# Moving the stores of the whole rows from SyncE's queue to ScalarE's queue in the node stage of a graph kernel

## The chip, the cores and the metric

The kernel runs on one NeuronCore of one Trainium2 chip. The metric is the device time of one execution in microseconds (us). Engines are named as the profile names them: PE is TensorE (PEld its weight loads), DVE is VectorE, ACT is ScalarE, POOL is GpSimd, SP is SyncE. SPq and ACTq are the instruction streams of SP and ACT where they issue DMAs.

## The reference, cut to what matters

The layer is a gated graph convolution over 16 images (called b) of 1024 nodes with 256 features.

```python
pre_u = jnp.einsum('bud,dk->buk', h_t, W1[:d])
pre_v = jnp.einsum('bvd,dk->bvk', h_t, W1[d:])
hidden = jax.nn.relu(pre_u[:, :, None, :] + pre_v[:, None, :, :] + b1)
S = jax.nn.sigmoid(jnp.einsum('buvk,ko->buvo', hidden, W2)[..., 0] + b2[0])
a_t = jnp.einsum('buv,bud->bvd', S * A_a, h_t)
m_t = jnp.einsum('uv,bud->bvd', A_m, h_t) * h_t
z_t = beta1 * h_t + beta2 * (jnp.einsum('bvd,de->bve', a_t, Wa) + ba) + beta3 * (jnp.einsum('bvd,de->bve', m_t, Wm) + bm)
```

`h_t` is the input x, float32 (16, 1024, 256), and `A_a` and `A_m` are both the sparse input adj, (1024, 1024). The gate S is wanted only where adj is not zero, so the kernel computes it for the edges alone.

## The kernel before, in words

The kernel has a short setup, then the **node stage** (from about 52 us to about 1,410 us of the profiled execution), the edge stage (to about 3,600 us), which gathers rows of pre_u and pre_v by matrix products with selection matrices and reduces them to gates, and a last stage that applies the gates. Only the node stage is touched by the change. Stages are parted by a barrier of all engines.

The node stage loops over the 16 images b. In each image a **row phase** comes first: for the eight tiles t of 128 nodes (g = 8b + t numbers them over all images)

- PE multiplies the turned image by both halves of W1 (w = 0 and 1, two products of 128x274 each, four instructions of the trace per half), L561, into the two banks `ring0` and `ring1`. It waits until the bank's last contents were copied out (`ring_free`).
- ACT copies bank 0 to `whole[:, g % RW, 0, :]` (L640), DVE adds the bias to bank 1 and writes `whole[:, g % RW, 1, :]` (L723). RW is 3: `whole` and `split` have three slots, so tile g may not be written before the stores of tile g - 3 have landed. Both engines wait for that on `rows_stored`.
- `high` on ACT (L631, a CAST in the trace) rounds the whole values to the high part of a pair; `low` on DVE (L678) takes the rest. They lag by one tile: ACT does copy(t), then high(t - 1); DVE does copy(t), low(t - 1), take_own(t - 2) (L684).
- POOL adds the two halves for the gates of nodes with themselves (L813) and takes some columns.
- SP, in `store_rows`, waits for low of the tile (`low_ready`) and issues four stores: rows_dram from `split` (256 KB, then 288 KB, L461) and whole_dram from `whole` (128 KB, then 144 KB, L464). Each of the four adds 16 to `rows_stored` of the slot; the slot is free at 64 more.

After the row phase come the products with the adjacency (L577, `wide`), among which the sorting of edges is placed by a fixed schedule (PE: `rank_pair` L520 and `index_pair`; DVE: `start_pick`, `pick_u`, `pick_v`, and in some images a scan, L741), then hWa (L599, copied by ACT at L647), the turning of the next image (L510), and the product with Wm (L616, added to `base` by DVE at L794). Then the next image's row phase starts. In its own stream SP stores the pick matrices (L475), fills gate_dram with zeros (L478), stores hWa and base (L481, L484: 1 MB each) and loads the image after next (L455, 1 MB), all in program order; the last two stand directly ahead of the next row phase's stores.

The order of all this is the order of the code; there is no planner.

Of the kernel before, what the change touches and what calls it, by code (L numbers as in the profile page):

```python
# [5 lines left out]
def gnn_edges_kernel(nc, x, adj, W1, b1, W2, b2, Wa, ba, Wm, bm, beta1, beta2, beta3, out):  # L6
# [17 lines left out]
    P = 128  # L24
# [18 lines left out]
    LATE = D // 2  # L43
    EARLY = CG - LATE
    EG = EARLY // GW
    E0 = B * LATE
# [16 lines left out]
    whole_rows = whole_dram.rearrange("(n w) k -> n w k", w=2)  # L63

    ctx = ExitStack()
    with ctx:
        def sb(name, shape, dt=fp32, scope=ctx):
            return scope.enter_context(nc.sbuf_tensor(name, shape, dt))
# [4 lines left out]
        def sem(name):  # L73
            return ctx.enter_context(nc.semaphore(name))

        def waits(eng, sem_, value):
            if not isinstance(value, int) or value > 0:
                eng.wait_ge(sem_, value)
# [49 lines left out]
        with ExitStack() as phase:  # L128
# [216 lines left out]
            RW, RPK = 3, 4  # L345
# [5 lines left out]
            whole = sb("whole", [P, RW, 2, CW], scope=phase)  # L351
# [37 lines left out]
            rows_stored = [sem(f"rows_stored{i}") for i in range(RW)]  # L389
# [37 lines left out]
            def pairs_of(b):  # L427
                return range(min(max(PER * (b - 2), 0), PAIRS), min(max(PER * (b - 1), 0), PAIRS))

            def tile_at(b):  # L430
                return FIRST.index(b) if b in FIRST else None
# [19 lines left out]
            with nc.Block() as block:  # L451
                @block.sync
                def _(sp):
                    def load_h(b):
                        sp.dma_start(h[b % 2][:], x[b, :, :].rearrange("(t p) d -> p t d", p=P)).then_inc(h_loaded[b % 2], 16)  # L455

                    def store_rows(b, t):
                        g = b * NT + t
                        sp.wait_ge(low_ready, g + 1)
                        for at, wd, first in ((b * LATE, LATE, 0), (E0 + b * EARLY, EARLY, LATE)):  # L460
                            sp.dma_start(rows_dram[t * P:(t + 1) * P, :, :, at:at + wd].rearrange("p w q k -> p (w q) k"),  # L461
                                         split[:, g % RW, :, :, first:first + wd].rearrange("p w q k -> p (w q) k")
                                         .bitcast(fp32)).then_inc(rows_stored[g % RW], 16)
                            sp.dma_start(whole_rows[t * P:(t + 1) * P, :, at:at + wd],  # L464
                                         whole[:, g % RW, :, first:first + wd]).then_inc(rows_stored[g % RW], 16)

                    for b in range(2):
                        load_h(b)
                    sp.wait_ge(zero_set, 1)
                    for b in range(B):  # L470
                        for t in range(NT):
                            store_rows(b, t)
                        for p_ in pairs_of(b):
                            sp.wait_ge(v_picked, unit_of[p_] + 1)
                            sp.dma_start(pick_dram[2 * p_:2 * p_ + 2, :, :].rearrange("h v k -> (h v) k"),  # L475
                                         pick[p_ % RPK][:].bitcast(fp32)).then_inc(pick_stored[p_ % RPK], 16)
                        for z in range(ZPER):
                            sp.dma_start(gate_fill[b * ZPER + z, :, :], zero[:]).then_inc(zero_stored, 16)  # L478
                        for i in range(2):
                            sp.wait_ge(ring_free[i], USES * b + NT + 2)  # L480
                        sp.dma_start(hWa_dram[b, :, :].rearrange("(t p) d -> p t d", p=P), hWa[:]).then_inc(hWa_stored, 16)  # L481
                        for i in range(2):
                            sp.wait_ge(ring_free[i], USES * (b + 1))
                        sp.dma_start(base_dram[b, :, :].rearrange("(t p) d -> p t d", p=P), base[:]).then_inc(base_stored, 16)  # L484
                        if b + 2 < B:
                            load_h(b + 2)
                    sp.wait_ge(slot_free, B * NT)
                    for w in range(2):
                        for q in range(HALVES):
                            sp.dma_start(rows_dram[:, w, q, L0:ROW].rearrange("(t p) b -> p t b", p=P),  # L490
                                         linear[:, :, w, q, :].bitcast(fp32)).then_inc(linear_stored, 16)
                        sp.dma_start(whole_rows[:, w, L0:ROW].rearrange("(t p) b -> p t b", p=P),
                                     linear_whole[:, :, w, :]).then_inc(linear_stored, 16)
                    for i in range(RW):
                        sp.wait_ge(rows_stored[i], 64 * ((B * NT - i + RW - 1) // RW))
                    sp.wait_ge(linear_stored, 16 * 2 * (HALVES + 1))
                    sp.wait_ge(zero_stored, 16 * ZROWS)
                    sp.wait_ge(hWa_stored, 16 * B)
                    sp.wait_ge(base_stored, 16 * B)
                    for i in range(RPK):  # L500
                        sp.wait_ge(pick_stored[i], 16 * ((PAIRS - i + RPK - 1) // RPK))
# [119 lines left out]
                @block.scalar  # L621
                def _(act):
                    def take_turned(b):
                        act.wait_ge(hT_psum, b * DT + 1)
                        nc.scalar.copy(hT[:, 0, :], wide[:, 0:N]).then_inc(hT_ready, 1)

                    def high(b, t):
                        g = b * NT + t
                        for i in range(2):
                            act.wait_ge(ring_free[i], USES * b + t + 1)  # L630
                        nc.scalar.copy(split[:, g % RW, :, 0, :], whole[:, g % RW, :, :]).then_inc(high_ready, 1)  # L631

                    take_turned(0)
                    for b in range(B):
                        for t in range(NT):
                            g = b * NT + t
                            act.wait_ge(ring_full[0], USES * b + t + 1)
                            waits(act, rows_stored[g % RW], 64 * (g // RW))
                            waits(act, slot_free, g - RW + 1)
                            nc.scalar.copy(whole[:, g % RW, 0, :], ring[:, 0:CW]).then_inc(ring_free[0], 1)  # L640
                            if t >= 1:
                                high(b, t - 1)
                        high(b, NT - 1)
                        waits(act, hWa_stored, b * 16)
                        for i in range(HT):
                            act.wait_ge(ring_full[i % 2], USES * b + NT + i // 2 + 1)
                            nc.scalar.copy(hWa[:, 2 * i:2 * i + 2, :].rearrange("p t k -> p (t k)"),  # L647
                                           ring[:, i % 2 * BANK:(i % 2 + 1) * BANK]).then_inc(ring_free[i % 2], 1)
                        second = tile_at(b + 1)
                        if second is not None:  # L650
                            act.wait_ge(rank_ready, second + 1)
                            if second >= 2:
                                act.wait_ge(ranked, unit_of[(second - 1) * NJ - 1] + 1)
                            for q in range(2):
                                nc.scalar.copy(cells[second % 2][q * UB:(q + 1) * UB, :, q * VB:(q + 1) * VB],
                                               rank[second % 2][q * UB:(q + 1) * UB, :].rearrange("p (j v) -> p j v", v=VB)).then_inc(cells_ready, 1)
                        if b + 1 < B:
                            take_turned(b + 1)
# [827 lines left out]
```

## Time and profile before

| | us |
|---|---|
| median of 3 runs | 4098.09 (4096.31 to 4102.22) |
| profiled execution | 4094.52 |
| its span | 4092.5 |
| PE busy in the span | 3611.8 (88%) |
| DVE busy | 2817.6 (69%) |
| ACT busy | 2061.1 (50%) |
| POOL busy | 1721.8 (42%) |

The mean granted TensorE clock was 0.946 of full speed. The shares are means over three different stages: ACT is nearly idle in the node stage (its digits in the page's forty slices are 0 to 1 for the first 14 slices) and busy in the edge stage. Instructions that issue DMAs are not counted as busy, so the load of a queue has to be read from the times of its issues. The chain that ended last on the page begins at 3,604 us, and says nothing of the node stage.

### The profile page before, as it was taken

How to read it: one execution, taken by the hardware profiler on the slowest of the kernel's cores; microseconds unless marked ns; L12 is line 12 of the kernel's file. 1: busy time of each engine (PE TensorE's matmuls, PEld its weight loads, DVE VectorE, ACT ScalarE, POOL GpSimd, SP SyncE). 2: the span in 40 equal slices, each digit the busy share in tenths (PEclk: the TensorE clock that was granted, in tenths of full speed). 3: DMA queues.
4: the chain of work that ended last, by engine and by line, in shares of the span. 5: the costliest groups of instructions: out<-in, count | busy, mean ns of one | idle time of the engine just before them, and what ended most of it. 6: DMA issues, size and time to landing. Idle time of an engine off the chain costs nothing. (4 is left out here: it accounts for less than half of the span.)

```text
span 4092.5 us, 57476 instructions
## 1 busy us (share of the span) xinstructions
PE 3611.8 (88%) x15258; PEld 2807.9 (69%) x15258; DVE 2817.6 (69%) x3940; ACT 2061.1 (50%) x13291; POOL 1721.8 (42%) x3056
## 2 busy tenths in 40 slices
PE   4977778887778749989999999999999999969999
PEld 3655445555545538877788788887888788858888
DVE  4454554555554248878888898998999898936665
ACT  0111111111111138988899899998999899900000
POOL 2222312222221216666576676666667576600000
PEclk9988889998989879999999999999999999979999
DMA  5555655655655595566645666566565665387665
GB/s 158 177 188 188 198 169 179 206 196 183 195 187 202 163 216 134 124 162 148 156 108 141 156 146 166 143 141 153 144 177 127 152 150 124 81 275 267 244 226 180
DMA packets 447582, 698.85 MB, mean 171 GB/s; under 512 B 45934, under 2 KB 358104, under 8 KB 425688
## 3 DMA queue, kind: packets, MB, share of 16 engines
q1 hardware_dynamic: 409232, 621.74, 54.0%
q0 software_dynamic: 21504, 56.57, 4.5%
q10 hardware_dynamic: 16512, 16.78, 1.2%
q8 instruction: 124, 2.03, 0.2%
q14 instruction: 210, 1.72, 0.1%
HBM read 451.57 MB, written 262.73 MB: 175 GB/s over the span
## 5 line engine op out<-in xcount | busy, mean ns | idle before, releaser
L1131 ACT ACTIVATE junk<-psum_a 128x128 f32<-128x128 f32 x6144 | 1619.3, 280 | 228.5 <-PE psum_a L1038 138.6
L1079 DVE TENSOR_REDUCE group_sum<-psum_d 128x64 f32<-128x1024 f32 (+1 forms) x1536 | 1439.0, 957 | 303.1 <-PE psum_d L1038 281.5
L1131 ACT ACTIVATION_READ_ACCUMULATOR junk<-psum_a 128x1 f32 x6144 | 1283.8, 209 | 0.1
L1037 PE MATMUL psum_d<-u_t,pk 128*128 128x512 f32 (+1 forms) x3072 | 1146.6, 379 | 52.5 <-DMA v_t<-rows_dram 32.0
L1038 PE MATMUL psum_d<-v_t,pk 128*128 128x512 f32 (+1 forms) x3072 | 1160.6, 378 | 0.0
L1190 POOL DMA_INDIRECT gate_dram<-gate,idx_all x512 | 505.9, 988 | 562.3 <-ACT gate L1119 451.6
L1037 PEld LDWEIGHTS psum_d<-u_t,pk 128*128 128x128 f32 x3072 | 582.1, 189 | 171.1 <-issue 43.8
L1037 PE MATMUL psum_a<-u_t,pk 128*128 128x512 f32 x1536 | 612.0, 398 | 58.0 <-ACT junk L1131 55.6
L1038 PEld LDWEIGHTS psum_d<-v_t,pk 128*128 128x128 f32 x3072 | 581.9, 189 | 111.6
L1038 PE MATMUL psum_a<-v_t,pk 128*128 128x512 f32 x1536 | 607.6, 396 | 0.0
L577 PE MATMUL wide<-adj_sb,h 128*128 128x512 f32 x1024 | 511.1, 622 | 0.0
L1445 PE MATMUL z_psum<-hWa_all,masked 128*128 128x256 f32 x2048 | 451.5, 384 | 43.6 <-DMA hWa_all<-hWa_dram 40.1
L1445 PEld LDWEIGHTS z_psum<-hWa_all,masked 128*128 128x128 f32 x2048 | 393.9, 193 | 101.2 <-DMA hWa_all<-hWa_dram 42.6
L813 POOL TENSOR_TENSOR own<-whole 128x274 f32<-128x274 f32 x128 | 90.9, 710 | 743.4 <-issue 707.1
L561 PE MATMUL ring<-W_k,hT 128*128 128x274 f32 x1024 | 293.8, 447 | 118.9 <-ACT whole L640 117.2
L647 ACT COPY hWa<-ring 128x512 f32<-128x512 f32 x64 | 37.5, 586 | 709.6 <-PE ring L599 709.6
L1037 PEld LDWEIGHTS psum_a<-u_t,pk 128*128 128x128 f32 x1536 | 291.1, 190 | 131.8 <-ACT junk L1131 59.6
L1427 DVE TENSOR_TENSOR masked<-raw,adj_b 128x2048 f32<-128x2048 f32 x64 | 234.3, 3664 | 210.3 <-PE z_psum L1445 131.7
L561 PEld LDWEIGHTS ring<-W_k,hT 128*128 128x128 f32 x1024 | 216.4, 217 | 192.6 <-ACT whole L640 136.1
L1079 DVE TENSOR_REDUCE late_sum<-psum_d 128x4 f32<-128x512 f32 x512 | 348.4, 680 | 0.0
L1038 PEld LDWEIGHTS psum_a<-v_t,pk 128*128 128x128 f32 x1536 | 291.4, 190 | 67.0
L577 PEld LDWEIGHTS wide<-adj_sb,h 128*128 128x128 f32 x1024 | 183.7, 201 | 146.7 <-issue 146.3
(189 smaller groups left out, 3379.2 us busy)
## 6 DMA issues: line engine op xcount, KB each, us to landing
u_t<-rows_dram SPq DMA_DIRECT2D x126, 1092.0 KB
gate_dram<-zero SPq DMA_DIRECT2D x128, 512.0 KB, 4.9
pk<-pick_dram SPq DMA_DIRECT2D x512, 128.0 KB, 2.7
raw<-gate_dram SPq DMA_DIRECT2D x64, 1024.0 KB, 4.8
v_t<-rows_dram SPq DMA_DIRECT2D x36, 1092.0 KB, 13.0
rows_dram<-split SPq DMA_DIRECT2D x128, 288.0 KB, 3.0
rows_dram<-split SPq DMA_DIRECT2D x128, 256.0 KB, 2.8
pick_dram<-pick SPq DMA_DIRECT2D x128, 256.0 KB, 2.0
```

The source lines that it names most:

```text
L561: last = nc.tensor.matmul(ring[:, w * BANK:w * BANK + CW], hT[:, c, t * P:(t + 1) * P], W1_k[:, c, w, :], start=(c == 0), stop=(c == DT - 1))
L577: last = nc.tensor.matmul(wide[:, c * N + n * BANK:c * N + (n + 1) * BANK], h[b % 2][:, t, c * P:(c + 1) * P], adj_sb[:, t, n * BANK:(n + ...
L647: nc.scalar.copy(hWa[:, 2 * i:2 * i + 2, :].rearrange("p t k -> p (t k)"), ring[:, i % 2 * BANK:(i % 2 + 1) * BANK]).then_inc(ring_free[i ...
L813: nc.gpsimd.tensor_tensor(own[g % 2][:], whole[:, g % RW, 0, :], whole[:, g % RW, 1, :], ALU.add).then_inc(own_part, 1)
L1037: nc.tensor.matmul(dst, pk[n % PKS][:, t * P:(t + 1) * P], u_t[k % 2][:, at:at + wd], start=True, stop=False)
L1038: return nc.tensor.matmul(dst, pk[n % PKS][:, SLOTS + t * P:SLOTS + (t + 1) * P], v_t[n % VG][:, at:at + wd], start=False, stop=True)
L1079: return nc.vector.tensor_reduce(out_, in_.rearrange("p (g k) -> p g k", g=g, k=wd), AX, ALU.add, apply_absolute_value=True)
L1131: last = nc.scalar.activation(junk[:, a % RING_A, k * LATE:(k + 1) * LATE], psum_a[a % RING_A][:, k * LATE:(k + 1) * LATE], ACT.Abs, accum ...
L1190: nc.gpsimd.indirect_dma_start(out=gate_dram[:, :], out_offset=bass.IndirectOffsetOnAxis(ap=at, axis=0), in_=gates, in_offset=None, bounds ...
L1427: nc.vector.tensor_tensor(masked[k % GM][:], raw[k % RAW][:].rearrange("p v b -> p b v"), adj_b[k % RAW][:].rearrange("p (a v) -> p a v", ...
L1445: last = nc.tensor.matmul(z_psum[b // 2][:, (b % 2) * D:(b % 2 + 1) * D], masked[k % GM][:, b, :], hWa_all[:, t, b, :], start=(t == 0 and ...
```

## The change

The two stores to whole_dram of each tile are taken out of SP's `store_rows` and put into ACT's `high`, right behind the copy that makes the high part. They carry the same bytes to the same place and add to the same semaphore. No wait is added: `high` has already waited for both halves of `whole`.

```diff
@@ -461,8 +461,6 @@
                             sp.dma_start(rows_dram[t * P:(t + 1) * P, :, :, at:at + wd].rearrange("p w q k -> p (w q) k"),
                                          split[:, g % RW, :, :, first:first + wd].rearrange("p w q k -> p (w q) k")
                                          .bitcast(fp32)).then_inc(rows_stored[g % RW], 16)
-                            sp.dma_start(whole_rows[t * P:(t + 1) * P, :, at:at + wd],
-                                         whole[:, g % RW, :, first:first + wd]).then_inc(rows_stored[g % RW], 16)
@@ -629,6 +627,9 @@
                         nc.scalar.copy(split[:, g % RW, :, 0, :], whole[:, g % RW, :, :]).then_inc(high_ready, 1)
+                        for at, wd, first in ((b * LATE, LATE, 0), (E0 + b * EARLY, EARLY, LATE)):
+                            act.dma_start(whole_rows[t * P:(t + 1) * P, :, at:at + wd],
+                                          whole[:, g % RW, :, first:first + wd]).then_inc(rows_stored[g % RW], 16)
```

On SP, at the head of the node stage (the load of image 1, then the stores of tiles 0 and 1 of image 0), before:

```order
L455 DMA h1<-in_x_dram 128x8x256
L461 DMA rows_dram<-split 512x1x128 [waits low_ready,zero_set]
L464 DMA whole_dram<-whole 256x1x128
L461 DMA rows_dram<-split 512x1x144
L464 DMA whole_dram<-whole 256x1x144
L461 DMA rows_dram<-split 512x1x128 [waits low_ready]
L464 DMA whole_dram<-whole 256x1x128
```

and after, in the same stream behind the load of an image, the stores of tiles 0 to 2 of image 1:

```order
L455 DMA h0<-in_x_dram 128x8x256
L461 DMA rows_dram<-split 512x1x128 [waits low_ready]
L461 DMA rows_dram<-split 512x1x144
L461 DMA rows_dram<-split 512x1x128 [waits low_ready]
L461 DMA rows_dram<-split 512x1x144
L461 DMA rows_dram<-split 512x1x128 [waits low_ready]
```

SP now issues two DMAs per tile where it issued four.

On ACT, in image 0, from the copy of tile 4 (slot 1) on, before:

```order
L640 COPY whole<-ring 128x274 [waits slot_free,rows_stored1,ring_full0]
L631 CAST split<-whole 128x2x274 [waits ring_free1,ring_free0]
L640 COPY whole<-ring 128x274 [waits slot_free,rows_stored2,ring_full0]
L631 CAST split<-whole 128x2x274 [waits ring_free1,ring_free0]
L640 COPY whole<-ring 128x274 [waits slot_free,rows_stored0,ring_full0]
```

and after (line numbers are those of the changed kernel: L641 is the copy, L629 the high part, L631 the store):

```order
L641 COPY whole<-ring 128x274 [waits slot_free,rows_stored1,ring_full0]
L629 CAST split<-whole 128x2x274 [waits ring_free1,ring_free0]
L631 DMA whole_dram<-whole 256x1x128
L631 DMA whole_dram<-whole 256x1x144
L641 COPY whole<-ring 128x274 [waits slot_free,rows_stored2,ring_full0]
L629 CAST split<-whole 128x2x274 [waits ring_free1,ring_free0]
L631 DMA whole_dram<-whole 256x1x128
L631 DMA whole_dram<-whole 256x1x144
L641 COPY whole<-ring 128x274 [waits slot_free,rows_stored0,ring_full0]
```

Two issues now stand between each high part and the next copy out of bank 0, and, for the last tile of an image, between high(6) and high(7).

## Rows read from the trace of the kernel before

**Rows 1.** Waits by releaser, 15 to 1440 us: total, times, longest.
```profile
PE ring L561 <- ACT whole L640: 117.2, 40, 6.7
ACT whole L640 <- DMA whole_dram<-whole: 110.7, 18, 8.0
```

**Rows 2.** Timeline of PE, row phase of image 6: start, us, what.
```profile
565.00 7.67 PE L561 MATMUL ring<-W_k,hT 128*128 128x274 f32 x32
578.34 5.81 PE L561 MATMUL ring<-W_k,hT 128*128 128x274 f32 x16 [5.66 <-ACT whole L640]
585.23 2.11 PE L561 MATMUL ring<-W_k,hT 128*128 128x274 f32 x8 [1.09 <-ACT whole L640]
```

**Rows 3.** Timeline of ACT, row phase of image 6, tiles 3, 5 to 7.
```profile
577.89 0.39 ACT L640 COPY whole<-ring 128x274 f32<-128x274 f32 x1 [7.01 <-DMA whole_dram<-whole]
...
584.79 0.39 ACT L640 COPY whole<-ring 128x274 f32<-128x274 f32 x1 [3.16 <-issue]
...
588.97 0.39 ACT L640 COPY whole<-ring 128x274 f32<-128x274 f32 x1 [3.24 <-issue]
589.25 0.65 ACT L631 CAST split<-whole 128x548 fp32r<-128x548 f32 x1
591.79 0.39 ACT L640 COPY whole<-ring 128x274 f32<-128x274 f32 x1 [1.88 <-issue]
```

**Rows 4.** Timeline of SP's issues, same row phase, tiles 0, 2, 3, 4.
```profile
570.13 0.53 SPq L461 DMA_DIRECT2D rows_dram<-split  x1
...
572.12 1.15 SPq L464 DMA_DIRECT2D whole_dram<-whole  x1
...
579.62 0.51 SPq L461 DMA_DIRECT2D rows_dram<-split  x1
...
581.53 0.67 SPq L464 DMA_DIRECT2D whole_dram<-whole  x1
...
584.00 1.56 SPq L464 DMA_DIRECT2D whole_dram<-whole  x1
...
586.26 0.64 SPq L464 DMA_DIRECT2D whole_dram<-whole  x1
...
589.00 0.66 SPq L464 DMA_DIRECT2D whole_dram<-whole  x1
```

**Rows 5.** DMA issues by line, 15 to 1440 us: count, KB each, us to landing.
```profile
rows_dram<-split SPq DMA_DIRECT2D x128, 288.0 KB, 3.0
...
whole_dram<-whole SPq DMA_DIRECT2D x128, 144.0 KB, 2.8
h<-in_x_dram SPq DMA_DIRECT2D x16, 1024.0 KB, 8.2
```

**Rows 6.** Stretches of that row phase: engines' busy us, PEclk, DMA share, GB/s.
```profile
568.00:578.00 10.00, 4.68 (x21) 3.49 (x19) 2.59 (x6) 2.08 (x5) 2.86 (x11) 0.86 1.08 305
578.00:582.00 4.00, 3.66 (x8) 2.83 (x9) 1.42 (x3) 1.77 (x4) 1.12 (x4) 0.50 0.65 176
582.00:592.00 10.00, 6.85 (x28) 4.83 (x28) 4.66 (x10) 2.09 (x5) 3.24 (x12) 0.99 0.74 222
592.00:600.00 8.00, 4.90 (x12) 1.90 (x10) 7.27 (x8) 1.27 (x3) 6.22 (x8) 0.95 0.98 292
```

**Rows 7.** Issues of whole_dram's and out_dram's stores: min/median/max ns.
```profile
L464 SPq DMA_DIRECT2D whole_dram<-whole x240: 513/657/1561, 136.8 to 1378.8; - x120
...
L1457 ACTq DMA_DIRECT2D out_dram<-z x8: 378/378/425, 3700.9 to 4084.6; - x8
```

**Rows 8.** Timeline of DVE at the end of that row phase.
```profile
593.75 0.72 DVE L678 TENSOR_TENSOR split<-whole,split 128x548 fp32r<-128x548 f32 x1
...
595.03 0.44 DVE L684 TENSOR_REDUCE own_abs<-own 128x17 f32<-128x272 f32 x1 [0.22 <-POOL own L813]
...
595.45 5.63 DVE L741 TENSOR_TENSOR_SCAN rank<-restart,edge 128x1024 f32<-128x1024 f32 x1
```

**Rows 9.** Waits by releaser, 100 to 1430 us, engine PE.
```profile
PE rankp L520 <- issue: 100.7, 12, 11.0
```

## The prediction

> **What bounds the kernel now.** The page's forty slices come first: PE's digits are 7 to 9 through the node stage with a few lower ones, ACT's are 0 and 1. So ACT has room on average, and what counts is where PE stands still. The waits by releaser show it: over the node stage PE waited 117.2 us in 40 stops for ACT to empty the first bank of the ring, and ACT itself waited 110.7 us in 18 stops for the stores of whole_dram [rows 1]. That is a chain through a slot: store lands, ACT copies, PE gets its bank. Over 16 images it is 7.3 us an image, and no change to the stores can bring more than that (and what the clock gives back).
>
> Then the timelines of one row phase, image 6, which the others resemble (their eight copies take 23.7 to 26.8 us from the first to the last; this one takes 25.7). PE can do four tiles in 7.67 us, 1.92 a tile [rows 2]. It does tiles 0 to 3 at that pace and stops, because tile 3 needs slot 0 again. ACT's copy of tile 3 comes at 577.89, and those of tiles 5, 6 and 7 at 584.79, 588.97 and 591.79 [rows 3]: (591.79 - 577.89) / 4 = 3.48 us a tile. In this stretch a tile's round is: the copy of tile t + 1, high and low of tile t, SP's four issues, the landing, the copy of tile t + 3. For tile 2 SP issued from 579.62 to the fourth issue at 581.53 and ACT went on at 584.79, 3.26 us behind that fourth issue; for tiles 3 and 4 the fourth issues at 586.26 and 589.00 were followed by the copies of tiles 6 and 7 after 2.71 and 2.79 us [rows 3, 4]. That is the landing time of these stores, 2.8 to 3.0 us [rows 5]. So in the second half of the phase SP's string of four issues and one landing set the pace.
>
> The first stop, tile 3's, is another matter. From 568 to 578 us the DMA engines were busy 1.08 of the time at 305 GB/s [rows 6]: 1 MB of base and 1 MB of the next image (landing 8.2 us after its issue [rows 5]) lie ahead of tile 0's stores. Transfers bound that stretch. From 578 to 592 the share was 0.65, then 0.74, and from 592 on 0.98 at 292 GB/s [rows 6].
>
> **The change, part by part.** Per tile SP loses two of four issues, at a median of 0.657 us each [rows 7]. ACT gets these two. The bytes stay the same.
>
> *Tile 3's stop: 0.* SP's string for tile 0 went from 570.13 to the fourth issue at 572.12 [rows 4]; without the two it would end 1.4 us earlier or so, but the slot came free at 577.9, since the data stood behind 2 MB. From below: with two queues feeding the same engines, tile 1's 272 KB of whole rows, issued on ACT early, may go ahead of tile 0's split rows: 0.28 MB at 292 GB/s is 0.95 us later. From above: the last of tile 0's issues is earlier by (572.12 - 570.13) - 0.6 = 1.4 us, and if all of it reaches the landing, the copy comes 1.4 us sooner. I take 0, since a full share stands in the row.
>
> *Tiles 5 to 7: 2.5 us sooner by the last copy.* Tile 2: the last issue is the second, near 580.2 instead of 581.53, 1.3 us less. Tile 3: the fourth issue stood at 586.26, with one of 1.56 us in the string [rows 4]; the second would be done issuing near 584.6, so 2.3 us sooner. Tile 4's string started late behind tile 3's, and ended at 589.00; without the backlog it follows low(4), which follows the earlier copies, and its second issue falls near 585.8, 3.2 us sooner. So by issues alone the copy of tile 7 could come at 588.6. But the transfers set a floor: a tile is 256 + 288 + 128 + 144 KB = 0.836 MB, at 292 GB/s 2.86 us [rows 6]. Four tiles at 2.86 instead of 3.48 save 4 x 0.62 = 2.5 us. I take this floor: the copy of tile 7 at 589.3. ACT's own load in this stretch is 0.28 for the copy (high follows it by that), 0.65 for high and 2 x 0.66 for the issues, 2.25 us a tile, below the 2.86. It is hidden by the wait for the slot.
>
> *The end of the phase: 0.9 us given back.* Now high(7) stood directly behind high(6). After the change two issues stand between. From the copy at 589.3: high(6) at 589.6 to 590.2, two issues to 591.5, high(7) to 592.2, low(7) to 592.9, against 594.47 (593.75 + 0.72 [rows 8]). So DVE, which was through at 595.45 (scan [rows 8]), is 1.6 us sooner and not 2.5. At an issue of 0.38, ACT's only one in the trace [rows 7], it would be 0.55 us better; at 1.56, SP's longest, 1.8 us worse.
>
> *What is late next.* In 14 of the 16 images PE's products after the row phase soon stop for the first rank_pair, which needs DVE's picks, and those come after DVE has finished the row phase (12 of these stops show as 100.7 us [rows 9]). So these images gain 1.6 us. Images 0 and 1 have no pairs, and PE goes straight on from its last tile: 2.5 us each. Behind that nothing is tied to SP's clock: the pick stores wait for DVE, the stores of hWa and base for ACT and DVE, so all shift together. The edge and last stages have none of it.
>
> *Sum:* 14 x 1.6 + 2 x 2.5 = 27 us. From the profiled execution's 4094.5 that makes 4067; the median of the runs was 3.6 us above that execution, so a median of **4070** is forecast. Its own range: with tile 3 0.95 us later, 0.65 and 1.55 an image, 12 us; with tile 3 1.4 us sooner and issues at 0.38, 3.6 us an image, 57 us. So 4041 to 4086.
>
> **What a page says against it.** The row shows a fourth issue behind a copy by 2.7 to 3.3 us and 1.9 us of issues before it in tile 2's string [rows 3, 4]. The Trainium skill, "DMA: Bandwidth & Descriptors", section "Issuing engines are not separate DMA queues", says that DMAs from all engines run on the same 16 DMA engines and that issuing on several saves only the sequencer's time, usually small beside the DMA. By it the gain is exactly the issue time and none of the transfer, and where transfers bound, it is nothing; the trace agrees for tile 3's stop (share 1.08) and disagrees with "small" for tiles 4 to 7.
>
> **The rivals.**
>
> *A. Landing absorbs it: no change.* The share from 582 to 592 was already 0.74, and 1.0 is near when the pace rises. If each landing grows by what the issue string loses (1.3 us on 3), the copies stay put, and only high(7)'s delay is left, hidden or not: 0 to +1.3 us an image if DVE waits. For it: 0.98 to 1.08 on both sides of the stretch. Against: 0.65 and 0.74 within it, that is 4.0 us idle of 14 [rows 6]. Time: 4094 to 4104, say 4098. The skill's rule above would give this for the whole phase.
>
> *B. ACT becomes the pacer: slower.* The place is the two issues between high(t - 1) and copy(t + 1). At p us per issue ACT needs 0.93 + 2p a tile. It reaches today's 3.48 at p = 1.27; from there on each tile is slower. SP shows such prices where the engines are full, 1.15 at tile 0 and 1.56 at tile 3 [rows 4], 1.56 being the longest of 240. With all of them at 1.56, a tile takes 4.05 us: 4 x 0.57 = 2.3 us, and high(7) 2.5 us later: 4.8 us an image, 77 in all, 4175. For it: the long ones. Against: the median 0.657, and 0.378 on ACT's queue [rows 7].
>
> *C. The first stop shrinks too.* If the second queue lets tile 0's stores through beside the 2 MB, the end of the above range holds: 57 us, 4041. For it: tile 0's whole rows no longer stand behind the image load in one queue. Against: the split rows still do, and the slot needs all four.
>
> The Trainium skill, same page, section "Queues, rings and completion order", says that each DMA engine goes round the queues that have work, packet by packet. By that rule ACT's stores do not stand behind SP's backlog, but tile 1's go before tile 0's split rows, which is the 0.95 us above; no run before shows two busy queues in this stage.
>
> **How the numbers follow.** Forecast 0.64, A 0.13, B 0.09, C 0.14. A measurement of this kernel tells a change from none at about 0.2%, 8 us. The forecast and C are faster by more than that (0.78; its own low end of 12 us too). A counts as no change, 0.12 with a little of it beyond; B as slower, with that rest, 0.10. The range: 4038 to 4100, from a little beyond C to A; it leaves out B and the tails.
>
> **What would show it.** Right: the copies of tiles 4 to 7 about 2.9 us apart in place of 3.5; PE's wait for ACT's copy down from 117 to some 75 to 85 us; a DMA share above 0.9 from 582 us of such a phase on; the first stop as long as before; ACTq issues near 0.65 us; low(7) only some 3.5 us behind the last copy where it was 2.7. Wrong: ACTq issues over 1.2 us with copies that wait for "issue" on ACT (B); landings of 4 us and more with the copies where they were (A); tile 3's copy less than 7 us behind tile 2's in most images (C); or a row phase that is shorter with the next one starting as late as before, which would mean that something later in the image, such as SP's zero fills or DVE's scan, sets the period.

## The result and the profile after

The changed kernel takes 4106.99 us (median of 20 runs, 4097.86 to 4116.33) against 4099.56 of the kernel before (20 runs). The ratio is 1.0019, with a 95% interval of 1.0011 to 1.0026: slower by 7 to 8 us where 28 us less were forecast. The profiled execution has a span of 4106.8 us and a granted clock of 0.944.

The node stage's end can be read from the gate of nodes with themselves, the first ACT work behind it: its L902 starts at 1430.6 us in the trace before and L903 at 1440.0 in the trace after. So 9.4 us of the 14.3 between the two spans arise in the node stage. The other 4.9 lie in stages that the change doesn't touch. The medians are only 7.4 apart, so these 4.9 can't be put down to the change.

The waits over the node stage (15 to 1440 us), answering to [rows 1]:

```profile
ACT whole L641 <- DMA rows_dram<-split: 208.0, 51, 9.0
...
PE ring L559 <- ACT whole L641: 130.7, 34, 7.7
```

and one more row of the kernel before, in the same window:

```profile
ACT whole L640 <- issue: 91.7, 34, 3.8
```

PE waits 130.7 us for ACT's copies, where it was 117.2. What frees the slot has changed: the last of a tile's four stores to land was one to whole_dram for all 128 tiles before, and is one of the split rows for all 128 now. The view of before puts only 18 of the stops to whole_dram and 34 to "issue"; the copies of tiles 5 to 7 in [rows 3] are such. By the trace's landings all 34 of these copies start 0.07 us behind the last store's landing, as the 18 do. Taken together ACT waited 202.4 us in 52 stops for its slot before, and 208.0 us in 51 after. The change is at work, and yet nothing is gained by it.

ACT's timeline in the row phase of image 6, issues included (compare [rows 3]):

```profile
568.86 0.39 ACT L641 COPY whole<-ring 128x274 f32<-128x274 f32 x1 [1.59 <-PE ring L559]
568.93 0.52 ACTq L631 DMA_DIRECT2D whole_dram<-whole  x1
569.27 0.65 ACT L629 CAST split<-whole 128x548 fp32r<-128x548 f32 x1
569.48 0.89 ACTq L631 DMA_DIRECT2D whole_dram<-whole  x1
570.70 0.39 ACT L641 COPY whole<-ring 128x274 f32<-128x274 f32 x1 [0.79 <-PE ring L559]
570.78 0.55 ACTq L631 DMA_DIRECT2D whole_dram<-whole  x1
...
571.36 0.69 ACTq L631 DMA_DIRECT2D whole_dram<-whole  x1
579.72 0.39 ACT L641 COPY whole<-ring 128x274 f32<-128x274 f32 x1 [8.08 <-DMA rows_dram<-split]
...
586.05 0.39 ACT L641 COPY whole<-ring 128x274 f32<-128x274 f32 x1 [2.72 <-PE ring L559]
...
590.77 0.39 ACT L641 COPY whole<-ring 128x274 f32<-128x274 f32 x1 [3.79 <-DMA rows_dram<-split]
...
592.63 0.39 ACT L641 COPY whole<-ring 128x274 f32<-128x274 f32 x1 [0.92 <-DMA rows_dram<-split]
```

Two things are to be seen. The issue, which stands behind the high part in the program, starts at 568.93, 0.34 us ahead of the high part's own start (569.27) and while the copy before it is still at work. And the step from the copy of tile 2 to that of tile 3 is 579.72 - 570.70 = 9.02 us, where it was 7.94. The landings of the trace say why: tile 1's whole rows, issued at 570.78 and 571.36, land at 577.56 and 578.80, and tile 0's split rows at 578.60 and 579.65, just ahead of the copy at 579.72. Before, all of tile 0's stores had landed by 577.83, and tile 1's whole rows at 579.08 and 580.63. It is so in every image from 1 to 14: tile 1's whole rows land ahead of the last of tile 0's stores after the change, and behind it before.

DMA issues by line over the node stage, count, KB, median us to landing (compare [rows 5]):

```profile
rows_dram<-split SPq DMA_DIRECT2D x128, 288.0 KB, 4.2
rows_dram<-split SPq DMA_DIRECT2D x128, 256.0 KB, 3.5
...
whole_dram<-whole ACTq DMA_DIRECT2D x128, 144.0 KB, 3.4
h<-in_x_dram SPq DMA_DIRECT2D x16, 1024.0 KB, 8.8
```

The split rows land 1.2 and 0.7 us later than before (3.0 and 2.8), the image load 0.6 later. The queues in the same stretch of the changed kernel (packets, MB, share of the 16 engines; q1 is SP's, q10 ACT's):

```profile
q1 hardware_dynamic: 229164, 226.54, 47.6%
q10 hardware_dynamic: 69632, 35.67, 8.5%
```

Together they hold the engines 56.1% of the time, about as long as q1 alone did before, 55.9%. No bandwidth was lost, it was dealt out otherwise.

The same stretches of image 6 as in [rows 6]:

```profile
568.00:578.00 10.00, 5.43 (x24) 4.12 (x22) 2.88 (x6) 1.97 (x4) 3.10 (x11) 0.90 1.05 299
578.00:582.00 4.00, 1.84 (x4) 1.48 (x5) 1.52 (x3) 0.94 (x2) 0.26 (x2) 0.50 0.85 222
582.00:592.00 10.00, 7.71 (x24) 5.64 (x24) 3.56 (x8) 2.81 (x6) 3.09 (x11) 0.79 0.78 232
592.00:600.00 8.00, 6.70 (x20) 3.26 (x18) 7.23 (x10) 1.58 (x3) 6.87 (x10) 1.00 0.88 262
```

PE's long stop in these stretches, and what it did next, from the same trace (compare [rows 2]):

```profile
580.16 8.76 PE L559 MATMUL ring<-W_k,hT 128*128 128x274 f32 x24 [6.73 <-ACT whole L641]
```

The share from 582 to 592 is 0.78, not above 0.9 as forecast, and the clock is lower there (0.79 beside 0.99). The stop before it was longer (6.73 us beside 5.66) and ended 1.8 us later.

To compare kernels, the starts of the eight copies out of bank 0 were read from each trace. The table has means over images 1 to 14, in us, from one profiled execution of each kernel (from act_not_1 on they are those of the experiments below): the steps between copies, their sum, and the distance from the last copy to the end of low(7).

| kernel | tile 2 to 3 | 3 to 4 | 4 to 5 | 5 to 6 | 6 to 7 | first to last | last copy to low(7)'s end |
|---|---|---|---|---|---|---|---|
| before | 7.77 | 2.81 | 3.62 | 3.93 | 3.03 | 24.98 | 2.81 |
| changed | 8.98 | 2.67 | 3.28 | 4.09 | 2.63 | 25.47 | 3.48 |
| act_not_1 | 8.05 | 2.83 | 3.03 | 4.23 | 2.54 | 24.50 | 3.62 |
| act_tail | 8.97 | 2.67 | 3.18 | 4.13 | 2.62 | 25.39 | 3.22 |
| sp_early | 8.06 | 2.84 | 3.12 | 3.51 | 3.09 | 24.44 | 2.78 |
| sp_ahead | 9.05 | 2.85 | 3.16 | 4.22 | 3.04 | 26.13 | 2.81 |
| sp_h_late | 4.96 | 2.89 | 3.60 | 3.26 | 3.39 | 21.91 | 2.68 |
| act_h_late | 5.09 | 2.32 | 3.74 | 3.34 | 3.37 | 21.68 | 3.23 |
| not1_h_late | 4.11 | 3.32 | 2.62 | 3.30 | 2.98 | 20.14 | 3.40 |
| early_h_late | 4.12 | 2.97 | 3.04 | 3.16 | 3.17 | 20.27 | 2.68 |
| ahead_h_late | 5.01 | 2.95 | 3.04 | 3.53 | 3.07 | 21.43 | 2.77 |
| early_h_base | 3.98 | 3.05 | 3.03 | 3.14 | 3.00 | 20.02 | 2.68 |

In images 0 and 15, whose row phases have no image load ahead of them, the changed kernel's trace is shorter: first to last copy 22.37 against 24.18 us, and 21.50 against 24.31. These are single phases, and other traces of the same code don't bear them out: image 15 takes 24.29 in act_tail and 24.21 in act_h_late, and image 0 takes 23.07 in act_h_late beside 22.88 in sp_h_late. Only the way from image 15's first copy to the gate is shorter in every one of them (80.5 to 80.7 us, where before and sp_h_late have 82.2 to 82.4).

### The profile page after: what moved, and what is told of

It is laid out like the page before. It is cut to its first block and busy times, and to the rows that moved or that the text cites. A ratio compares the mean times of both kernels' runs of the same rounds, so it can differ in the third digit from the quotient of the medians.

```text
span 4106.8 us, 57476 instructions
## 1 busy us (share of the span) xinstructions
PE 3611.7 (88%) x15258; PEld 2809.3 (68%) x15258; DVE 2817.5 (69%) x3940; ACT 2058.1 (50%) x13291; POOL 1726.6 (42%) x3056
## 5 line engine op out<-in xcount | busy, mean ns | idle before, releaser
L559 PE MATMUL ring<-W_k,hT 128*128 128x274 f32 x1024 | 294.5, 450 | 132.0 <-ACT whole L641 130.7
```

What stands on the lines that cost most here:

```text
L559: last = nc.tensor.matmul(ring[:, w * BANK:w * BANK + CW], hT[:, c, t * P:(t + 1) * P], W1_k[:, c, w, :], start=(c == 0), stop=(c == DT - 1))
```

## The experiments

Theory O: the order in which transfers reach the engines decides. A later tile's whole rows, in a queue with nothing ahead, pass an earlier tile's split rows, and the slot is freed by the last of four. Theory Q: a second busy queue costs by itself. Theory I: the issues on ACT hold up ACT's own work. Four kernels against O, Q and I came first.

**act_not_1: tile 1's whole rows go back to SP.**

```diff
 # in high(), ACT
+if t != 1:
     act.dma_start(whole_rows[...], whole[...])
 # in store_rows(), SP, behind each store of the split rows
+if t == 1:
+    sp.dma_start(whole_rows[...], whole[...])
```

> The changed kernel, but the whole rows of tile 1 of each image are stored by SyncE behind that tile's split rows, as before the change; all other whole rows by ScalarE. Theory O (order): the step from the copy of tile 2 to that of tile 3, mean 8.9 us in images 1 to 14 of the changed kernel and 7.7 before, grew because tile 1's whole rows, 272 KB in a queue of their own, pass tile 0's split rows, which wait behind 2 MB in SyncE's queue. Then this step comes back to 7.7 us or less, and the time falls by 10 to 17 us against the changed kernel, to about 4092. Theory Q (a second busy queue slows every transfer, whatever its order): tile 0's whole rows are still in the second queue, the step stays at 8.5 us or more and the time at 4107. Theory I (the issues on ScalarE hold up its copies): no change of this step either.

Measured: 4088.57 us (11 runs), ratio to before 0.9979 [0.9970, 0.9988], apart from the changed kernel's 1.0019 [1.0011, 1.0026]. The step fell from 8.98 to 8.05, not quite to 7.7. ACT's copies of tiles 2 and 3 of image 6:

```profile
566.45 0.39 ACT L645 COPY whole<-ring 128x274 f32<-128x274 f32 x1 [0.78 <-PE ring L562]
574.41 0.39 ACT L645 COPY whole<-ring 128x274 f32<-128x274 f32 x1 [7.02 <-DMA rows_dram<-split]
```

One pair of stores in eight, moved back, turns the change from a loss into a gain of about 9 us. The 18 us between it and the changed kernel are a little more than the 10 to 17 expected. Q fails here: tile 0's whole rows are still in the second queue, and by Q the step would have stayed at 8.5 us or more. I is not tested by the edit, though the expectation says so: tile 1's two issues stood right ahead of the copy of tile 3, and the edit took them off ACT. It is the changed kernel's trace that rules I out for this step: the second of these issues is over at 572.05, and the copy starts at 579.72, when the split rows have landed. The 0.28 us by which the step stays above the kernel before are not explained.

**act_tail: ACT stores tile 6 behind high(7).**

```diff
-high(b, 7)                # with the stores of tile 6 behind high(b, 6)
+high(b, 7)
+store_whole(b, 6); store_whole(b, 7)
```

> The changed kernel, but ScalarE issues the stores of tile 6 only behind the high part of tile 7, with those of tile 7. The end of low(7) behind the copy of tile 7 was on average 0.64 us later than before the change. If two issues in front of high(7) are its cause, this distance goes back by 0.5 to 0.7 us in each image and the time falls by 8 to 11 us, to about 4097. Rival: the delay comes from the transfers (VectorE's copy waits for the slot, or the stores still queue), then the distance and the time stay (4107). The step of tile 3 stays at 8.9 us in both.

Measured: 4106.56 us (11 runs), ratio 1.0014 [1.0004, 1.0024], not told apart from the changed kernel. Its trace is of its slowest run (4113.85), so only the shape is used. The distance fell from 3.48 to 3.22, less than half of what was expected. In the images whose last step is 2.8 us or more it is back at 2.68; in those with a shorter last step it mostly stays at 3.5 to 3.9, since there DVE waits for PE's second bank. Three of the ten images with a shorter last step are at 2.68 too. So ACT's issues are one part of the longer tail; the other is that ACT's copy now comes up to 1.8 us ahead of DVE's, which waits for PE's second bank. The kernel before has this in images 1, 3 and 14 alone. The time did not fall by the 8 to 11 us expected. Where the issues are the cause, the changed kernel's trace shows it (image 4, from the copy of tile 7 on):

```profile
411.32 0.39 ACT L641 COPY whole<-ring 128x274 f32<-128x274 f32 x1 [2.04 <-DMA rows_dram<-split]
411.42 0.52 ACTq L631 DMA_DIRECT2D whole_dram<-whole  x1
411.60 0.65 ACT L629 CAST split<-whole 128x548 fp32r<-128x548 f32 x1
411.97 1.00 ACTq L631 DMA_DIRECT2D whole_dram<-whole  x1
413.06 0.65 ACT L629 CAST split<-whole 128x548 fp32r<-128x548 f32 x1 [0.81 <-issue]
```

High(7) starts 1.46 us behind high(6), where it was 0.55 us before, with no issue between them.

**sp_early: one queue, tile order, whole rows ahead of the wait for low.**

```diff
 for t in range(NT):
+    store_whole(b, t)     # SP: waits for ring_free of both banks, then the two stores
     store_rows(b, t)      # SP: waits for low_ready, now the two stores of split rows
```

> One queue, SyncE's, as before the change, but the two stores of a tile's whole rows are issued ahead of the wait for its low part (they wait for both halves of whole instead); the order of the tiles in the queue is kept. Theory O: nothing can pass, so the step of tile 3 is 7.7 us or less, and only two issues stand between low and the landing, so tiles 5 to 7 come 0.5 to 2.5 us earlier per image: 4060 to 4090. Theory Q: the same, since there is one queue. Rival L (transfers alone set the pace, the string of issues is worth nothing): steps and time as before the change, 4096 to 4103.

Measured: 4085.3 us (5 runs), ratio 0.9964 [0.9951, 0.9978], 13 us faster than the 4098.31 beside it, within the expected range. Copies of image 6, tiles 2 to 4:

```profile
563.93 0.39 ACT L647 COPY whole<-ring 128x274 f32<-128x274 f32 x1 [0.79 <-PE ring L568]
571.99 0.39 ACT L647 COPY whole<-ring 128x274 f32<-128x274 f32 x1 [7.12 <-DMA rows_dram<-split]
574.82 0.39 ACT L647 COPY whole<-ring 128x274 f32<-128x274 f32 x1 [1.90 <-PE ring L568]
```

The step of tile 3 is 8.06 us, the same as act_not_1's 8.05 with two queues, and 0.3 above the kernel before; the later steps are 0.8 us shorter together. So a shorter string of issues behind low is worth something, but far less than the forecast had.

**sp_ahead: the same with tile t + 1's whole rows ahead of tile t's split rows.**

```diff
+store_whole(b, 0)
 for t in range(NT):
-    store_whole(b, t)
+    if t + 1 < NT: store_whole(b, t + 1)
     store_rows(b, t)
```

> One queue, SyncE's, but the whole rows of tile t + 1 are issued ahead of the split rows of tile t: the order in which the changed kernel's two queues bring them, without the second queue. Theory O: the step of tile 3 grows as in the changed kernel, to 8.5 us or more, since 272 KB stand ahead of tile 0's split rows; time 4095 to 4110. Theory Q: the step stays at 7.7 us and the time is that of the kernel with early stores in tile order or better.

Measured: 4112.07 us (6 runs), ratio 1.0035 [1.0023, 1.0047], 27 us slower than sp_early in the same comparison, a little above the expected range. Copies of tiles 2 and 3 of image 6:

```profile
571.99 0.39 ACT L649 COPY whole<-ring 128x274 f32<-128x274 f32 x1 [0.78 <-PE ring L570]
581.08 0.39 ACT L649 COPY whole<-ring 128x274 f32<-128x274 f32 x1 [8.16 <-DMA rows_dram<-split]
```

The step of 9.05 us is the changed kernel's 8.98, made in a single queue. The edit does two things at once: it puts 272 KB ahead of tile 0's split rows, and it puts two issues ahead of them in SP's string, so that the second split store starts 1.86 us behind low and not 0.58 (means over images 1 to 14). At the first stop the later issue can't be the cause: in the kernel before, the last store of tile 0 starts 2.04 us behind low, and it lands 7.55 us behind low, where sp_early has 7.84 and sp_ahead 8.83. That settles the first stop for O. The rest of the 27 us is not order in the DMA engines: 0.71 us an image are in the step of tile 6, where the second split store of tile 3 starts 0.86 us later and takes as long to land (3.20 and 3.29 us).

**sp_h_late and act_h_late: the 1 MB image load behind the row stores,** in the kernel before and in the changed one.

```diff
 # SP, image b
-if b + 2 < B: load_h(b + 2)          # last in image b, ahead of the next row phase
+if 1 <= b and b + 1 < B: load_h(b + 1)   # behind the eight row stores of image b
```

> The kernel before, but the 1 MB load of a coming image is issued behind the eight row stores of the next row phase, not in front of them. Theory O says that tile 3's stop is the time that base's 1 MB, the image's 1 MB and tile 0's stores need; without the image the step of tile 3 falls from 7.7 us to about that of the row phases that have no load (5.0 and 5.5 us in images 0 and 15), so 2.3 us in 14 images, 32 us in all: 4066, unless the later load holds up the pick stores. Rival (the stop is a latency, not bytes): no change.

> The changed kernel with the same late load. In images 0 and 15, which have no load in front, the changed kernel's row phase was 1.8 and 2.8 us shorter than before. Theory O: with fewer bytes ahead of tile 0's split rows there is less to pass and the change gains in every image: 1 to 2.5 us an image against the kernel before with the late load, so 4030 to 4055. Theory Q (a second busy queue costs by itself) and theory I (ScalarE's issues cost): it stays slower than that kernel, 4070 to 4080.

Measured: sp_h_late 4045.65 us (4 runs), ratio 0.9883 [0.9868, 0.9898]; act_h_late 4051.93 (4 runs), ratio 0.9884 [0.9869, 0.9899]. The late load is worth 51 us, not the 32 expected: the step of tile 3 lost 2.81 us, the later steps 0.25 together, the end of the phase 0.13, and the way from there to the next image's first copy 0.36 (57.70 beside 58.06): 3.55 us in 14 images, 50 us. PE's stop in image 6 lasted 2.52 us, where it was 5.66 [rows 2], and the clock's fall is shorter: it was granted 0.58 in the 4 us behind the stop and then 1.00 (sp_h_late, the stretch of the stop and the two behind it):

```profile
546.00:553.00 7.00, 4.62 (x21) 3.43 (x19) 2.79 (x6) 2.28 (x6) 2.81 (x11) 1.00 0.81 251
553.00:557.00 4.00, 3.86 (x10) 3.01 (x11) 1.36 (x4) 1.57 (x4) 1.12 (x4) 0.58 0.80 244
557.00:567.00 10.00, 6.99 (x29) 4.85 (x28) 4.77 (x10) 2.65 (x6) 3.35 (x12) 1.00 0.77 235
```

The expectation for act_h_late was wrong in what it claims, though 4051.93 lies in its range: the change gains nothing there, the two ratios are the same. The load is gone, but base's 1 MB still stands ahead of tile 0's split rows, and the end of the phase still costs ACT's share (3.23 us against 2.68).

**early_h_late and early_h_base: the early stores in tile order with the late load; then base's store in four parts as well.**

```diff
-sp.dma_start(base_dram[b, :, :]..., base[:]).then_inc(base_stored, 16)
+for i in range(HT):       # each waits for its ring_free
+    sp.dma_start(base_dram[b, 2 * i * P:(2 * i + 2) * P, :]..., base[:, 2 * i:2 * i + 2, :]).then_inc(base_stored, 16)
```

> One queue, whole rows ahead of the wait for low in tile order, and the late load. If the gains add up, 13 us from the early stores and 32 from the load: about 4053. Against the changed kernel with the late load it tells what the second queue is worth once nothing stands ahead: theory O says the same within 8 us.

> The kernel of the last run, with the 1 MB store of base issued in four parts as VectorE finishes them, of which three begin before the row phase, where the DMA engines stood idle. Theory O: about 0.75 MB less in front of tile 0's stores, so the step of tile 3 falls by up to 2 us more and the time by 10 to 30 us, to about 4030. Rival: the step is by then bound by the round of issues and the landing, about 4.5 us, and only half of that comes.

Measured: early_h_late 4020.75 us (5 runs), ratio 0.9820 [0.9807, 0.9834]; early_h_base 4017.2 (5 runs), ratio 0.9809 [0.9795, 0.9822]. The gains more than add up: 76 us, where 13 and 51 had been measured apart. The expectation of 4053 was wrong, and so was the other one, that early_h_late would be within 8 us of act_h_late: it is 31 us faster. The excess lies in the step of tile 3. The early stores alone made it 0.29 us longer and the late load alone 2.81 shorter, together they make it 3.65 shorter (4.12 beside 7.77), 1.13 us an image more than the sum. In early_h_late PE's stop of image 6 is 1.99 us and the clock does not fall:

```profile
534.18 7.67 PE L568 MATMUL ring<-W_k,hT 128*128 128x274 f32 x32
543.84 2.11 PE L568 MATMUL ring<-W_k,hT 128*128 128x274 f32 x8 [1.99 <-ACT whole L647]
```

```profile
539.00:544.00 5.00, 3.01 (x14) 2.16 (x13) 2.14 (x5) 1.54 (x4) 2.19 (x8) 1.00 0.90 265
544.00:548.00 4.00, 3.28 (x14) 2.39 (x15) 2.31 (x5) 1.27 (x3) 1.12 (x5) 1.00 0.99 290
```

Base's store in parts brought a step of 3.98 us instead of 4.12, where up to 2 us less were expected, and its time is not told apart. The rival of that expectation holds: by then the step is the round of copy, high and low, issues and landing, and no longer a matter of bytes ahead. In early_h_late tile 0's low ends 3.97 us behind its copy, and its last store lands 3.89 us behind low. Both kernels, early_h_late and early_h_base, beat the kernel before by 1.8 to 1.9%.

**ahead_h_late and not1_h_late: order and queue told apart once more, with the late load.** The edits are those of sp_ahead and act_not_1.

> One queue with the whole rows of tile t + 1 ahead of the split rows of tile t, and the late load: beside the changed kernel with the late load (step of tile 3 5.1 us, copies spanning 21.7 us, 4052) and the one queue in tile order (4.1, 20.3, 4021). Theory O (order): step near 5.0, a span of 21 to 22 us and 4035 to 4055, with one queue. Theory Q (the second queue itself costs): like the one queue in tile order, step near 4.1 and 4015 to 4028.

> The changed kernel with tile 1's whole rows back on SyncE and the late load. Theory O: the step of tile 3 falls from 5.1 to 4.1 to 4.4 us and the time by 8 to 14 us from the changed kernel with the late load, to 4036 to 4044; what is then left to 4021 is the end of the phase, where high(7) stands behind ScalarE's issues (0.5 us an image, 8 us), and the later tiles. Theory Q: step at 5 us or more, 4047 to 4055.

Measured: ahead_h_late 4040.2 us (4 runs), ratio 0.9863 [0.9846, 0.9881], step 5.01; not1_h_late 4027.17 (5 runs), ratio 0.9832 [0.9819, 0.9846], step 4.11. So with the late load the step is 5.0 to 5.1 us wherever tile 1's whole rows stand or pass ahead of tile 0's split rows, in one queue or two, and 4.1 wherever they don't, in one queue or two. But the two 5.0s are made in different ways. With one queue (ahead_h_late) the second split store of tile 0 starts 1.45 us behind low, beside 0.58 in early_h_late, and takes as long to land, 3.35 and 3.31 us: SP's string of issues is what is longer. With two queues (act_h_late) it starts 0.60 us behind low, as in not1_h_late, and takes 4.25 us to land instead of 3.28: here the transfers pass. So ahead_h_late does not copy what the second queue does, and it is not1_h_late that speaks against Q.

not1_h_late gained more than expected (4036 to 4044). Over all 16 images its copies span 324.7 us in sum, early_h_late's 324.8; its distances from last copy to low(7) are 11.0 us longer in sum, and its time is 6 us longer, with intervals that overlap.

A fourth slot for whole and split would have tested the round itself; no run has one.

## Why the prediction was wrong, point by point

- **Tile 3's stop: "I take 0". This is the step that failed.** It measured +1.21 us an image (8.98 against 7.77), 17 us in 14 images, and without them the change would have gained, as act_not_1 does. The mechanism was in the text, as the bound from below, at 0.95 us; the error was to take the middle for the reason "a full share stands in the row". With the share at 1.08 the bytes ahead decide, and the change put 272 KB ahead. act_not_1, sp_ahead and the order of the landings show that it is these bytes.
- **Tiles 5 to 7: "2.5 us sooner by the last copy". Mis-sized, and in microseconds the larger miss (25 us in 14 images).** From the copy of tile 3 to that of tile 7 it took 13.39 us before and 12.67 after: 0.7 us. The floor of 2.86 a tile was used as if it would be reached; sp_early, where nothing passes, gets 0.8 us. Much of what the string of issues lost came back as landing. For tiles 2, 3 and 4 the last store to land started 1.4 to 1.6 us less behind low than before, and took 0.5, 1.1 and 0.9 us longer to land (means over images 1 to 14). Of what was left, some went to copies that then waited for PE. That was rival A, at 0.13, and for these steps it was mostly right. The backlog of issues that was added up came from one image, with a single issue of 1.56 us in it; that image's 3.48 us a tile is 3.35 in the mean. The Trainium skill, "DMA: Bandwidth & Descriptors", section "Issuing engines are not separate DMA queues", says that starting DMAs on several engines saves only the sequencer's time, usually small. The trace agrees here, with 0.7 us of 13.4.
- **The end of the phase: "0.9 us given back". The size was about right** (0.67 us to the end of low(7)), partly by luck, since there are two causes and only one was named: the issues, and DVE's wait for PE's second bank. The first issue does not wait for the high part's end, it runs beside it, so high(7) starts 0.6 to 1.0 us later behind high(6) than before in seven of the eight images where DVE hardly waits, and not 1.3; in image 1, with an issue of 2.04 us, it is 2.0 us.
- **What is late next: right.** From the end of the row phase's DVE work to the next image's first copy it is 58.06 us before and 57.86 after; the phase's loss passes through.
- **Rival B (ACT paces) did not happen:** ACT's issues have a median of 0.63 us and the copies wait for DMA. Rival C did not either.
- **The sum.** Images 1 to 14: first to last copy +0.49, to DVE's end +0.58 more, then -0.20, 0.87 us each and 12.2 in all; image 0 gained 1.5 us to the next image's first copy and image 15 gained 1.7 to the gate; the first copy came 0.4 later. 12.2 - 3.2 + 0.4 = 9.4, as read at the stage's end. Beside the forecast 27 us less, 17 come from tile 3's step and 25 from the steps behind it, and the rest gives some 5 back. A gain near the forecast 1.6 to 2.5 us stands only in these two images, and image 0's is not repeated in other traces (65.3 us to the next image's first copy in the changed kernel and in sp_h_late alike).

## What to carry to other kernels

In this kernel a buffer is freed by the last of several transfers and the DMA engines are full, and there a store moved to a queue of its own did not become cheap. It went ahead of what stood in the old queue, and the buffer that was wanted next was freed later. Ask first what stands ahead of the transfer that frees the slot: here a load of 1 MB, which in the kernel before landed 52 to 74 us ahead of its first use, was worth 51 us, seven times what the moved stores cost. With that load out of the way, two issues ahead in the same queue cost time by themselves (0.87 us, ahead_h_late). A bound that the argument names and the rows support should be taken as the value, not as an end of the range.

## What the runs showed of the hardware that was not expected

- A DMA issue on ACT starts before the instruction ahead of it in the program does: 0.34 and 0.18 us before the start of the high part that precedes it (568.93 and 569.27; 411.42 and 411.60). The instruction behind it has to wait for the issue: high(7) of image 4 starts at 413.06, the issue before it ends at 412.97.
- The DMA engines' time is about the same with one queue or two for the same bytes (55.9% and 47.6% + 8.5%); what differs is which of them land first.
- PE's granted clock in the four us behind a stop: 0.50, the lower level of 1.2 GHz, behind one of 5.66 us (kernel before), 0.58 on average behind one of 2.52 (sp_h_late), and 1.00, 2.4 GHz, behind one of 1.99 (early_h_late), all in image 6. Over the 16 images of sp_h_late, with stops of 2.5 to 3.2 us, it was 1.00 in six and 0.50 to 0.65 in ten. Whether this is part of the 12 us by which two gains of 13 and 51 made 76 is not shown: the excess is in the step of tile 3, and the way from the row phase's end to the next image's first copy is 58.01 us in early_h_late, no shorter than the 58.06 before.
